# Recurrence of a fused block: input sums of eight steps in two wide products, seeds through the identity, recurrent products of 32 columns

## The reference

```python
xw = jnp.einsum('ntd,dh->nth', x, Wx) + b
def step(prev_h, xw_t):
    next_h = jnp.tanh(xw_t + prev_h @ Wh)
    return (next_h, next_h)
_, hs = jax.lax.scan(step, h0, jnp.swapaxes(xw, 0, 1))
```

## Time and profile before

| | us |
|---|---|
| median of 3 runs | 1146.18 (1141.81 to 1150.68) |
| the profiled execution's span, first to last instruction | 1136.0 |
| PE busy | 1042.3 (92%) |
| DVE busy | 580.7 (51%) |
| ACT busy | 547.1 (48%) |
| POOL busy | 311.8 (27%) |
| recurrence, about 12.0 to 516.1 of the span | 504.1 |

### The profile page before, as it was taken

One profiled execution on the slowest core, in us unless ns is written; L12 is line 12 of the kernel. 1 busy time (PEld: TensorE's weight loads), 2 busy tenths in 40 slices (PEclk: granted clock), 3 DMA queues, 4 the chain that ended last, 5 costly groups with the idle time before them and its releaser, 6 DMA issues.

```text
span 1136.0 us, 62532 instructions
## 1 busy us (share of the span) xinstructions
PE 1042.3 (92%) x26280; PEld 782.3 (69%) x26280; DVE 580.7 (51%) x1954; ACT 547.1 (48%) x1956; POOL 311.8 (27%) x308
## 2 busy tenths in 40 slices
PE   8899999999999999997798999999998999999994
PEld 5566666666666666666685444457888999999994
DVE  2333333333333333336585898998754655645641
ACT  2333333333333333337685777673344665665652
POOL 2111111111011111012240005437602455455455
PEclk7999999999999999999899999999999999999998
DMA  2121221122433333203861001104325566566644
GB/s 86 50 75 63 74 75 63 60 74 66 47 42 41 42 41 44 28 10 58 184 133 41 1 0 62 46 32 145 141 66 177 127 148 156 124 148 149 131 61 47
DMA packets 85349, 89.63 MB, mean 79 GB/s; under 512 B 8657, under 2 KB 71654, under 8 KB 85298
## 3 DMA queue, kind: packets, MB, share of 16 engines
q1 hardware_dynamic: 70706, 71.87, 25.2%
q0 software_dynamic: 14592, 17.10, 9.0%
HBM read 56.82 MB, written 33.96 MB: 80 GB/s over the span
## 4 chain that ended last, share of the span: by engine, by line
PE 64%; DVE 11%; ACT 9%; issue 7%; POOL 5%; DMA 2%; SPq 1%; POOLq 1%; DVEq 0%; ACTq 0%
PE ps L521 18%; PE ps L793 14%; PE ps L807 7%; DVE tok L1139 7%; PE ps L659 7%; ACT zt L859 6%; PE ps L500 4%; PE ps L503 3%; PE ps L709 2%; PE ps L490 2%; POOL slots_in L446 2%; PE ps L581 2%; PE ps L566 2%; PE ps L718 2%; POOL big L420 1%
## 5 line engine op out<-in xcount | busy, mean ns | idle before, releaser
L1139 DVE STREAM_TRANSPOSE tok<-zt 128x32 f32<-128x32 f32 x1024 | 159.6, 194 | 331.3 <-ACT zt L859 310.7
L859 ACT ACTIVATE zt<-ps 128x32 f32<-128x32 f32 x1024 | 146.2, 195 | 332.3 <-PE ps L521 332.3
L521 PE MATMUL ps<-wh,tok 128*8 128x64 f32 x8192 | 212.1, 222 | 43.4 <-DVE tok L1139 1.9
L500 PE MATMUL ps<-wx,xst 128*8 128x64 f32 x8320 | 217.7, 221 | 1.1 <-issue 1.1
L521 PEld LDWEIGHTS ps<-wh,tok 128*8 128x8 f32 x8192 | 118.1, 88 | 123.9 <-DVE tok L1139 110.3
L465 POOL DMA_INDIRECT out<-arena,dest x80 | 127.6, 1595 | 98.8 <-ACT arena L1017 79.6
L503 PE MATMUL ps<-brow,tri 1*8 1x64 f32 x4160 | 153.9, 217 | 0.7 <-issue 0.7
L500 PEld LDWEIGHTS ps<-wx,xst 128*8 128x8 f32 x8320 | 145.0, 91 | 4.7 <-issue 2.4
L793 PE MATMUL ps<-xgT_hi,ew_hi 128*128 128x320 f32 (+1 forms) x384 | 118.7, 309 | 4.1 <-DVE spare L1281 1.6
L793 PE MATMUL ps<-xgT_hi,ew_lo 128*128 128x320 f32 (+1 forms) x384 | 119.0, 310 | 0.0
L793 PE MATMUL ps<-xgT_lo,ew_hi 128*128 128x320 f32 (+1 forms) x384 | 118.2, 308 | 0.0
(11 more groups left out here) (206 smaller groups left out, 1754.6 us busy)
## 6 DMA issues: line engine op xcount, KB each, us to landing
ring<-k_pad SPq DMA_DIRECT2D x64, 256.0 KB, 6.2
slots_in<-mid SPq DMA_DIRECT2D x16, 645.0 KB, 3.3
mid<-slots_in SPq DMA_DIRECT2D x16, 645.0 KB, 4.2
arena<-in_ex_down SPq DMA_DIRECT2D x16, 384.0 KB, 3.2
arena<-in_ex_gate SPq DMA_DIRECT2D x16, 352.0 KB, 4.7
arena<-in_ex_up SPq DMA_DIRECT2D x16, 352.0 KB, 5.9
xst<-in_x_steps SPq DMA_DIRECT2D x66, 64.0 KB, 1.8
xtok<-in_x_tok SPq DMA_DIRECT2D x16, 256.0 KB, 2.7
```

Of the source, the lines that this page charges most:

```text
L500: nc.tensor.matmul(sums_at(bank, t)[Q * j:Q * j + B], xst[:, bank, k, t], wx[:, k, j * W:(j + 1) * W], start=t < 2 and k == 0, stop=False, ...
L521: last = nc.tensor.matmul(sums_at(bank, t)[Q * j:Q * j + B], hring[:, (n - 1) % (2 * G), k, 0:B], wh[:, k, j * W:(j + 1) * W], start=False ...
L859: nc.scalar.activation(zt[:, n % 2, half], sums_at(n // G, n % G)[:, half], ACT.Tanh).then_inc(s_zt, 1)
L1139: nc.vector.transpose(hring[:, n, k], zt[:, n % 2, k * Q:(k + 1) * Q]).then_inc(s_h, 1)
```

## The change

The input sums (with bias) of eight steps are now formed by two products of 64 rows (8 steps x 8 of the batch) by 256 columns into bank 5 (`inputs_summed`, at t = 1 and t = 2). DVE adds `brow`, which now holds the bias in 64 rows, and writes them to `xw` in SBUF (`inputs_out`, after steps 5 and 13). Before a step's recurrent products, `seed` puts its rows into the accumulators: stationary is the slice of the identity that picks the step's 8 rows, moving are 32 columns of `xw`. Recurrent products have 32 columns, half 0 of every block in banks 0 and 1, half 1 in banks 2 and 3 (by parity of t), and each half signals `s_sum` by itself; ACT waits for each. `loads` is issued by ACT, `ident` moves from `late` to `first`, `tri` the other way. `xw` lies in `spare`, whose upper 64 partitions are cleared once.

```diff
-        brow = sb("brow", [1, D])
+        brow = sb("brow", [G * B, D])
+        xw = spare[:].rearrange("p (n d) -> p n d", n=2)
...
-        first = ((wx, wx_d), (tri, tri_d), (brow, b_rec_d))
+        first = ((wx, wx_d), (ident, ident_d), (brow, b_rec_d))
...
-        def sums_at(group, t):
-
-            return ps[:, 2 * group + t % 2, t // 2 * W:(t // 2 + 1) * W]
+        def sums_at(t, half):
+
+            return ps[:, 2 * half + t % 2, 0:Q]
...
-            for dst, src in loads:
-                sp.dma_start(dst[:], src).then_inc(s_const, 16)
...
-            def xpart(bank, t):
-
-                for k in range(C):
+            def inputs_summed(bank, c):
+
+                return nc.tensor.matmul(ps[0:G * B, 5, 0:D], xst[:, bank, c].rearrange("p t b -> p (t b)"), wx[:, c], start=c == 0, stop=c == C - 1)
+
+            def seed(bank, t):
+
+                for half in range(2):
                     for j in range(J):
-                        nc.tensor.matmul(sums_at(bank, t)[Q * j:Q * j + B], xst[:, bank, k, t], wx[:, k, j * W:(j + 1) * W],
-                                         start=t < 2 and k == 0, stop=False, skip_group_check=True, tile_position=(0, Q * j))
-                for j in range(J):
-                    last = nc.tensor.matmul(sums_at(bank, t)[Q * j:Q * j + B], tri[0:1, 1, 0:B], brow[:, j * W:(j + 1) * W],
-                                            start=False, stop=False, skip_group_check=True, tile_position=(0, Q * j))
-                return last
+                        nc.tensor.matmul(sums_at(t, half)[Q * j:Q * j + B], ident[:, B * t:B * t + B], xw[:, bank, j * W + half * Q:j * W + half * Q + Q],
+                                         start=True, stop=False, skip_group_check=True, tile_position=(0, Q * j))
...
-                        for j in range(J):
-                            last = nc.tensor.matmul(sums_at(bank, t)[Q * j:Q * j + B], hring[:, (n - 1) % (2 * G), k, 0:B], wh[:, k, j * W:(j + 1) * W],
-                                                    start=False, stop=True, skip_group_check=True, tile_position=(0, Q * j))
-                    last.then_inc(s_sum, 1)
-                    if t == 0:
+                        for half in range(2):
+                            for j in range(J):
+                                last = nc.tensor.matmul(sums_at(t, half)[Q * j:Q * j + B], hring[:, (n - 1) % (2 * G), k, 0:B], wh[:, k, j * W + half * Q:j * W + half * Q + Q],
+                                                        start=False, stop=k == C - 1, skip_group_check=True, tile_position=(0, Q * j))
+                            if k == C - 1:
+                                last.then_inc(s_sum, 1)
+                    if t < G - 1:
+                        seed(bank, t + 1)
+                    else:
+                        pe.wait_ge(s_xin, 2 * i + bank + 2)
+                        seed(1 - bank, 0)
+                    if t == 1:
                         pe.wait_ge(s_xs[1 - bank], 16 * i + 16 + 16 * bank)
-                    last = xpart(1 - bank, t)
-                    if t == G - 1:
-                        last.then_inc(s_xdone, 1)
+                        inputs_summed(1 - bank, 0)
+                    if t == 2:
+                        inputs_summed(1 - bank, 1).then_inc(s_xdone, 1)
...
+            for dst, src in loads:
+                act.dma_start(dst[:], src).then_inc(s_const, 16)
...
-                    act.wait_ge(s_sum, 2 * G * i + n + 1)
-                    for k in range(C):
-                        half = slice(k * Q, (k + 1) * Q)
-                        nc.scalar.activation(zt[:, n % 2, half], sums_at(n // G, n % G)[:, half], ACT.Tanh).then_inc(s_zt, 1)
+                    for half in range(2):
+                        act.wait_ge(s_sum, 4 * G * i + 2 * n + half + 1)
+                        nc.scalar.activation(zt[:, n % 2, half * Q:half * Q + Q], sums_at(n, half), ACT.Tanh).then_inc(s_zt, 1)
...
+            def inputs_out(done, bank):
+
+                dve.wait_ge(s_xdone, done)
+                nc.vector.tensor_tensor(xw[0:G * B, bank], ps[0:G * B, 5, 0:D], brow[:], ALU.add).then_inc(s_xin, 1)
...
+                    if n % G == 5:
+                        inputs_out(2 * i + n // G + 2, 1 - n // G)
```

More of the change, by code:

```diff
@@ L244, in build @@
         s_late = sem("s_late")
+        s_xin = sem("s_xin")
         s_tile = [sem("s_tile%d" % n) for n in range(NSLOT)]
@@ L255, in build @@
                  (dt_bc, dt_bc_d), (c_q, c_q_d), (d_k, d_k_d), (consts, consts_d), (iota_t, iota_t_d), (rows_to, rows_to_d))
-        late = ((ident, ident_d), (h0g, h0_gate), (gw, gate_w), (gb, gate_b), (rw, router_w), (rb, router_b),
+        late = ((tri, tri_d), (h0g, h0_gate), (gw, gate_w), (gb, gate_b), (rw, router_w), (rb, router_b),
                 (resets, resets_d), (iota_e, iota_e_d))
@@ L493, in kernel_sums @@
                     last.then_inc(s_kmm, 1)
-            def xpart(bank, t):
-                for k in range(C):
+            def inputs_summed(bank, c):
+                return nc.tensor.matmul(ps[0:G * B, 5, 0:D], xst[:, bank, c].rearrange("p t b -> p (t b)"), wx[:, c], start=c == 0, stop=c == C - 1)
+            def seed(bank, t):
+                for half in range(2):
                     for j in range(J):
-                        nc.tensor.matmul(sums_at(bank, t)[Q * j:Q * j + B], xst[:, bank, k, t], wx[:, k, j * W:(j + 1) * W],
-                                         start=t < 2 and k == 0, stop=False, skip_group_check=True, tile_position=(0, Q * j))
-                for j in range(J):
-                    last = nc.tensor.matmul(sums_at(bank, t)[Q * j:Q * j + B], tri[0:1, 1, 0:B], brow[:, j * W:(j + 1) * W],
-                                            start=False, stop=False, skip_group_check=True, tile_position=(0, Q * j))
-                return last
+                        nc.tensor.matmul(sums_at(t, half)[Q * j:Q * j + B], ident[:, B * t:B * t + B], xw[:, bank, j * W + half * Q:j * W + half * Q + Q],
+                                         start=True, stop=False, skip_group_check=True, tile_position=(0, Q * j))
             for _ in range(WARM):
                 keep_up(512)
-            pe.wait_ge(s_ps0, 1)
             pe.wait_ge(s_first, FIRST_LOADED)
             pe.wait_ge(s_xs[0], 16)
-            for t in range(G):
-                last = xpart(0, t)
-            last.then_inc(s_xdone, 1)
+            inputs_summed(0, 0)
+            inputs_summed(0, 1).then_inc(s_xdone, 1)
+            pe.wait_ge(s_ps0, 1)
+            pe.wait_ge(s_xin, 1)
+            seed(0, 0)
             def steps(i, bank):
@@ L1114, in _ @@
             nc.vector.memset(ctmp, 0.0).then_inc(s_x1, 2)
+            nc.vector.memset(xw[G * B:P], 0.0)
+            def inputs_out(done, bank):
+                dve.wait_ge(s_xdone, done)
+                nc.vector.tensor_tensor(xw[0:G * B, bank], ps[0:G * B, 5, 0:D], brow[:], ALU.add).then_inc(s_xin, 1)
+            dve.wait_ge(s_first, FIRST_LOADED)
+            inputs_out(1, 0)
             dve.wait_ge(s_state, STATE_LOADED)
@@ L1470 @@
         "wh": rec(L0_cond_Wh),
-        "b_rec": np.asarray(L0_cond_b)[None],
+        "b_rec": np.broadcast_to(np.asarray(L0_cond_b), (G * B, D)),
         "a_bc": np.broadcast_to(a_log, (P, NST)),
```

1 line of the change is left out of this document (removed).

## The result

| | before | changed |
|---|---|---|
| median of 4 runs, us | 1145.66 (1141.81 to 1150.68) | 1166.81 (1157.80 to 1178.43) |
| ratio, changed to before | | 1.0179, 95% interval 1.0129 to 1.0229 |
| span of the profiled execution, us | 1136.0 | 1155.7 |

The change made the kernel 1.8% slower. Its four executions lie in two pairs, 1157.80 and 1159.25, 1174.37 and 1178.43, so the median stands for neither; the profiled one is the fastest, and against the lower pair alone the kernel is 1.1% slower. The forecast was 1180 us, with 1143 to 1233 as its own range: the direction is right and the size is 13 us too high. Its reasons are only partly right, which the sum alone would have hidden.

A forecast was written before the change was run, and what follows sets the result against it. The recurrence's ring of latencies, 0.97 us a step, was taken as the bound. Steps averaging 1.062 us, half clock included (+39), and the start (-3) gave 1172 on 1136.0; with 10 to the median 1182, put at 1180; range 1143 to 1233.

The forecast's parts named there:

- (a): Recurrent products of 32 columns, half 0 with its own signal: ring 0.052 us a step shorter, 0.974 to 0.922.
- rival C: A pass of 32 columns costs what one of 64 does: a step takes 1.05 us, time 1216; chance 0.07.
- the four rounds of the first half of h just fill that: In a recurrence step, the second half of h arrives about 0.11 us later; four rounds take 0.116.
- (b): Seeds replace L500 and L503 in the recurrence's pause: 0.349 us of PE per step instead of 0.56 plus shape changes.
- (c): Two wide products in every eight steps: 1.05 us of PE, next product 0.13 late in 4 of 16 steps.
- (d): inputs_out on DVE at n = 5 and 13, about 0.42 us each, costs nothing.
- (e): At the start, the nine loads come first on ACT's queue: -3 us (0 to -4).
- (f): TensorE's clock falls in sparse runs of the recurrence, 5 of 16 steps at half clock: 1.062 us average, +39 us.
- the prediction's own sign: Wrong if the clock holds at full with PE busy near 60%, or wide steps are no longer than the others.
- Rival A: The clock holds in the recurrence: -19 to -16 us, time 1128; chance 0.19.
- Rival D: The ring doesn't shorten, as the signal per half costs ACT what it saves; clock holds: about 1147 us; chance 0.07.
- The sum's 10 us from the profiled span to the median: The runs' median, 1146.2, lies 10 us above the profiled span, 1136.0; the same was added to 1172, giving 1182.

The follow-up runs named there:

- 64-column kernel: Changed kernel with seeds and recurrent products back at 64 columns, one bank and one signal per step; 1181.35 us, ratio 1.0356.
- two semaphores: Changed kernel with DVE signalling the two halves of h on two semaphores, so both waits of a PE step use one number; 1149.23 us, ratio 1.0053.
- half-major: Changed kernel with recurrent products issued half by half: half 0 with k = 0 and 1, then half 1 with both; 1159.92 us, ratio 1.0136.
- one signal: Changed kernel with ACT waiting for both halves' products before its first tanh; 1200.18 us, ratio 1.0492.

## Why the prediction was right or wrong

**The ring, (a).** Right: a round of four 32-column tiles is 0.029 us, as taken, the bound of 0.056 and with it rival C are out. Right too that the added wait on ACT costs nothing; the signal per half is worth more than counted. Wrong: "the four rounds of the first half of h just fill that", so that k = 1 starts at 0.117. The array was free and the second half of h was signalled at +0.058, but the loads came at +0.153, because a register computation of PE's sequencer stands between, and eight products are issued ahead of it where it had been four. Last product of half 0 at +0.211 instead of 0.145 forecast; the ring gained 0.010 instead of 0.052. That is +0.04 by 511 = 20 us on the side of slower, and it is the term that failed. Half of what was missing came back when the computation was taken away (0.942); the other half is a tanh that starts 0.02 later behind its product than the sum had it, for a cause that isn't known. The order of the instructions in the section on the change shows the REGISTER_ALU at just that place; the sum costed the eight products by the array alone.

**The seeds, (b),** are hidden, as forecast: PE waits 0.45 us a step for the transposes.

**The wide products, (c).** Right, and splitting them bore it out: 1.070 and 1.089 for a forecast of 1.05. Over the sparse steps that is 0.11 and 0.13, in 4 of 16 steps 0.03 a step, as the sum had it. The gain beside it didn't come: the average is 0.994 instead of 0.954.

**inputs_out, (d).** Right: DVE takes 0.40 for it, for 0.42.

**The start, (e).** -1.6 for -3. The first transpose now waits for other things than rows_to: an exponential of ACT for DVE's dta_q, at 9.96.

```profile
9.96 0.31 ACT L862 ACTIVATE lam<-dta_q 128x128 f32<-128x128 f32 x1 [0.43 <-DVE dta_q L1136]
...
10.57 0.33 DVE L1156 STREAM_TRANSPOSE tok<-zt 128x32 f32<-128x32 f32 x2 [0.64 <-ACT zt L868]
```

**The clock, (f).** The place and the prices were right, the share was not. Behind the first 33 us it fell at the end of the sparse run, each time in n = 8, and came back in the steps with wide products. One fall, at 297.2:

```profile
297.09 0.62 PE L523 MATMUL ps<-wh,tok 128*8 128x32 f32 x32 [0.38 <-DVE tok L1156]
...
297.67 0.30 ACT L868 ACTIVATE zt<-ps 128x32 f32<-128x32 f32 x2 [0.78 <-PE ps L523]
...
298.90 0.62 PE L523 MATMUL ps<-wh,tok 128*8 128x32 f32 x32
...
300.62 0.42 PE L523 MATMUL ps<-wh,tok 128*8 128x32 f32 x32
```

A wide step at half clock is 1.80 (forecast 1.86), a sparse one 1.07 (1.11), and a fall costs 1.34 to 1.41 us. But behind the start there were three falls in 32 turns, not one in each: 4 us, and 12.1 with the stalls and half-clock steps of the first 33 us, instead of the 55 (0.108 by 511) of the sum. The sum had taken a falling clock in every sparse run, from three stretches before with 28% to 53% busy; a sparse run is busy for 63% of its time, 0.61 us a step where 0.52 was counted. By the prediction's own sign, a clock that holds at full with PE busy near 60%, this part was wrong. That it was near shows in the 64-column kernel, where the clock fell fifteen times.

Rival A, the clock holds, is therefore nearly what happened, and yet the kernel isn't faster, because its 1128 stood on the ring of 0.92. Rival D, 0.99 on average with the clock held and 1147, has the right steps for a reason that is wrong; nobody had a case for the late loads. The rule beside A (TensorE: Matmul & The Clock Gate, "Why this matters for your kernels", in the Trainium skill), that drops come from idle gaps between bursts of matmuls, doesn't cover what happened: in the kernel of 64 columns the clock fell fifteen times where PE's products show at most 0.45 us of idle time ahead of them in the steps before each fall, those of the one at 116 here:

```profile
114.19 0.41 PE L521 MATMUL ps<-wh,tok 128*8 128x64 f32 x16 [0.45 <-DVE tok L1153]
...
115.16 0.41 PE L521 MATMUL ps<-wh,tok 128*8 128x64 f32 x16 [0.45 <-DVE tok L1153]
...
116.14 0.61 PE L521 MATMUL ps<-wh,tok 128*8 128x64 f32 x16 [0.45 <-DVE tok L1153]
```

**What was not in the sum.** The convolution stage, which the change doesn't touch, took 95.5 us before and 101.7 after. The waits in it, before (516.2 to 611.2) and changed (530.5 to 632.1):

```profile
PEld ps L581 <- issue: 9.4, 6, 3.5
...
PEld ps L566 <- issue: 6.8, 10, 2.0
```

```profile
PEld ps L574 <- issue: 13.1, 12, 3.5
...
PEld ps L589 <- issue: 7.7, 7, 3.5
```

PE's waits for nothing that a semaphore shows went from 16.2 to 20.8 us in these two lines, and the clock of the stage from 0.95 to 0.92. In the other kernels whose recurrence stays loaded the stage took 96.9 to 109.2, without an order that follows their edits, and 125.1 in one, the kernel with split products and two semaphores. Its page and waits (502.5 to 627.5):

```profile
q8 instruction: 40, 0.66, 0.2%
```

```profile
PEld ps L577 <- issue: 23.3, 11, 9.8
PEld ps L592 <- issue: 9.8, 9, 2.8
```

That execution took 1155.51 us, while the kernel's other eleven took 1131.93 to 1139.85. It loaded 40 blocks, nine more than the 31 of the kernel with the split products alone, and they arrived in this stage, which has a loop on PE too. That the nine blocks made this execution 20 us longer is argued from these numbers, since none of the other eleven was profiled. Whether they are also behind the 6 us of the table, and behind the changed kernel's two executions of 1174 and 1178, no run isolated: this stays open, with 1 to 14 us in the usual executions, and it is as large as the recurrence's own differences. The sum's 10 us from the profiled span to the median, too, came out by chance: the changed kernel's profiled execution has 2 us outside its span, and the other 9 are its median's place between the two pairs.

So the forecast landed near by luck. Two errors met in the recurrence: 20 us of ring gain that didn't come, and 43 us of half-clock steps (55 less 12) that didn't come either. Together they leave the forecast 23 us above its +16.4; the start's 1.4 and the 5 us outside the recurrence take some of that back.

## What to carry to other kernels

In a ring of latencies, cost PE's sequencer beside its array: a wait whose number must be computed starts behind all products issued ahead of it, and a semaphore for each of two signals, so that one number serves both, gave 0.02 us a step. Work that already lies in a pause is free; gathering it into one long product makes it a block that can overrun the pause (here 0.11 to 0.13 us), and cutting that product into pieces that fit gave back 14 us. Before thinning out PE's work, or filling it up again, look at the granted clock and at the number of instructions in a loop's turn: one kept or lost 27 us here, the other cost 600.

## What the runs showed of the hardware

- More PE work can make a kernel faster: seeds issued twice took the 64-column kernel from 1181.35 to 1144.80 us, 27 us of it by way of the granted clock in the recurrence. The stage behind it was 7 us shorter too, which is within what that stage varies by here.
- A loop whose turn has up to 1648 recorded PE instructions stays loaded; with 1879 and 2008 it is loaded again in every turn, about 2.2 us a block of 16 KB (5.10 MB in 311).
- An execution 20 us longer than the others of its kernel had loaded 40 instruction blocks, where a kernel with the same products loaded 31, and its convolution stage took 125.1 us for 96.9 to 109.2 elsewhere.
- A weight load follows the signal it waits for by 0.042 us, unless a register computation queued behind eight products stands ahead of its wait: then it came 0.095 behind it (+0.153 for a signal at +0.058).
- fp32 passes of 32 columns on column tiles go on scaling: 194 ns for one and 0.029 us a round of four, against 222 and 0.056 with 64.
- A tanh that waits for a product of 32 columns starts 0.255, 0.260, 0.278 or 0.290 us behind that product's start in four kernels that differ in what PE issues around it (changed, half-major, two semaphores, one signal). The 0.035 us between them is unexplained. With 64 columns it is 0.286, of which 0.027 is the longer pass.
